# Nonlocal attention and the second MoE's dispatch in one block

## The reference

```python
x = x + nonlocal(_ln_c(x))      # theta, phi, g: 1x1 convolutions 256 -> 128; phi and g on the 2x2 max-pooled image
    m1 = softmax(theta1 @ phi1)                # 4096 queries x 1024 keys
    m2 = m1 @ gi1                              # 4096 x 128
    m4 = conv1x1(m2.reshape(128, 64, 64), wz_w, wz_b)
t = t + moe(_ln_t(t))           # logits = t @ Wg + bg, the two largest, softmax over the two
    out += w_e * (gelu(t @ W1[e] + b1[e]) @ W2[e] + b2[e])     # W1: 256 x 1024, W2: 1024 x 256
```

## Time and profile before

| | us |
|---|---|
| median of 3 runs | 2480.7 (2469.35 to 2482.45) |
| the profiled execution | 2486.87, its span 2485.1 |
| layer1_start | about 1670 to 1758 |
| nonlocal_attention | about 1759 to 1893 |
| dispatch of MoE 1 | about 1894 to 2028 |
| experts of MoE 1 | about 2035 to 2438 |
| combine, output | to 2485 |

### The profile page before, as it was taken

How to read it: one execution, slowest core, us unless ns; L and a number is a source line. 1 busy time by engine, 2 the same in 40 slices (tenths; PEclk the granted TensorE clock), 3 DMA queues, 4 the chain that set the end, 5 groups by cost and what they waited for, 6 DMA issues and landing times. The chain is left out here.

```text
span 2485.1 us, 83832 instructions
## 1 busy us (share of the span) xinstructions
PE 2015.4 (81%) x28694; PEld 1524.5 (61%) x28695; DVE 2062.4 (83%) x3713; ACT 1732.2 (70%) x2708; POOL 790.9 (32%) x604
## 2 busy tenths in 40 slices
PE   6749999999999999999996208856896229999994
PEld 3327666666666766666664206643684129999992
DVE  5779999999999999999997646759797457777775
ACT  5569999999999999999984415537686335555551
POOL 3432124241431331231440553430364532222220
PEclk9869999999999999999997559985997559999996
DMA  2013323232323232323232233442112341111116
GB/s 81 1 34 89 84 77 89 72 92 70 92 71 91 71 90 71 90 72 89 73 85 84 87 131 104 116 126 95 45 68 84 112 135 51 48 47 47 51 44 209
DMA packets 285209, 202.98 MB, mean 82 GB/s; under 512 B 153395, under 2 KB 259846, under 8 KB 284870
## 3 DMA queue, kind: packets, MB, share of 16 engines
q1 hardware_dynamic: 271168, 163.57, 22.8%
q0 software_dynamic: 12960, 35.73, 3.9%
q10 hardware_dynamic: 998, 2.62, 0.3%
HBM read 68.98 MB, written 108.60 MB: 71 GB/s over the span
## 5 line engine op out<-in xcount | busy, mean ns | idle before, releaser
L595 DVE TENSOR_TENSOR plow<-prob 128x1024 f16<-128x1024 f32 (+1 forms) x1024 | 1127.1, 1171 | 3.7 <-ACT prob L506 3.7
L506 ACT ACTIVATE prob<-scores 128x1024 f32<-128x1024 f32 x1024 | 999.5, 1025 | 88.9 <-PE scores L638 58.5
L658 PEld LDWEIGHTS outp<-vs,prob 128*128 128x128 bf16 x7680 | 515.3, 98 | 279.8 <-issue 219.9
L658 PE MATMUL outp<-vs,prob 128*128 (+1 forms) x7680 | 603.6, 193 | 25.0 <-DVE plow L595 12.4
L638 PE MATMUL scores<-qT,kT 128*128 (+1 forms) x2048 | 610.6, 380 | 7.5 <-DMA kT<-shift_rows 2.7
L660 PE MATMUL outp<-vs,plow 128*128 (+1 forms) x7680 | 601.2, 193 | 0.0
L660 PEld LDWEIGHTS outp<-vs,plow 128*128 128x128 f16 x7680 | 502.8, 97 | 57.9
L448 POOL TENSOR_TENSOR osum<-osb 128x128 f32<-128x128 f32 x64 | 269.9, 4217 | 783.4 <-DVE rec L600 783.4
L1476 POOL DMA_INDIRECT expert_rows<-m1eyo,m1edest x71 | 108.0, 1521 | 304.5 <-DVE m1eyo L1448 275.5
L1347 PE MATMUL m1eph<-m1exT,m1ew1c 128*128 128x128 f16 x3408 | 203.4, 220 | 0.3 <-ACT m1exT L1384 0.3
L1347 PEld LDWEIGHTS m1eph<-m1exT,m1ew1c 128*128 128x128 f16 x3408 | 194.5, 98 | 1.0 <-ACT m1exT L1384 0.5
(11 more groups left out here) (393 smaller groups left out, 3335.4 us busy)
## 6 DMA issues: line engine op xcount, KB each, us to landing
sorted_rows<-zero SPq DMA_DIRECT2D x128, 522.0 KB, 4.7
staged<-qk SPq DMA_DIRECT2D x73, 128.0 KB, 2.3
m0exr<-sorted_rows SPq DMA_DIRECT2D x71, 130.5 KB
...
```

Source lines behind the costliest of these rows:

```text
L506: act.activation(prob[g % PBUF][:, :], scores[g % 2][:, :], ACT.Exp, scale=1.0 / (QK_SCALE * QK_SCALE)).then_inc(prob_ready, 1)
L595: dve.tensor_tensor(l[:, 0:n], p[:, 0:n], high(p)[:, 0:n], ALU.subtract).then_inc(low_ready, 1)
L658: pe.matmul(to, high(prob[g % PBUF])[:, cols], v, start=(g == 0 and i == 0 and j == 0), stop=False, skip_group_check=True)
```

## The change

Attention and dispatch become one block, `nonlocal_and_dispatch`. No loop: all 39 ticks (32 and 7 behind them) are written out. A row tile's result is now multiplied by the reciprocal in ACT (`image`, out of PSUM), and the reciprocal is taken by DVE straight behind the exponential (`invert`); `project(r-1)` stands where `project(r)` would, behind `scores`; the bias of the projection is two more one-row matmuls instead of POOL's addition. As soon as four token tiles are final they pass through the dispatch steps: `scales` (the root now by DVE in 13 linked operations instead of ACT), `normed`, `prepare`, `turn_row`, `take`, `mult` (8 matmuls instead of 4), `first_choice`, `second_choice`, `rank`, `places` and POOL's two sends for each tile, 4 to 11 ticks behind the attention. W2 now lies in the room that the attention's operands use, so its 16 parts are loaded and halved only after the last projection, three in each of the ticks 33 to 37 and one in tick 38. The MoE's `b1`, gate and bias loads go to the block's start; `experts` and `combine_experts` stay.

```diff
-def nonlocal_attention(nc, qh, ql, kh, kl, gh, gl, zw, zb_dram, ident32, tok, stats, w1_dram, w1):
+def nonlocal_and_dispatch(nc, qh, ql, kh, kl, gh, gl, zw, zb, prob, pth, ptl, tok, stats, consts, ...):
...
+        TICKS = range(NT + 7)
+        due = lambda r, i: (r - i) // TG if (r - i) % TG == 0 and 0 <= (r - i) // TG < NGR else None
+        w2_before = lambda r: min(NW2, max(0, 3 * (r - NT))) if r < NT + 6 else NW2
...
+            for i in range(NW2):                      # sync
+                if i < KB:
+                    sp.wait_ge(w1_high, 4 * (E_N - 1) + 2 * i + 2)
+                elif i == KB:
+                    sp.wait_ge(w1_split, NT)
+                else:
+                    sp.wait_ge(w2_split, i - 2)
...
+            for r in TICKS:                           # vector
+                if r + LOOKED < NT:
+                    maxima(r + LOOKED)
+                if 1 <= r <= NT:
+                    add(r - 1)
+                if r + 1 < NT:
+                    invert(r + 1)
+                g = due(r, 10)
+                if g is not None:
+                    places(g)
+                g = due(r, 6)
+                if g is not None:
+                    prepare(TG * g)
+                g = due(r, 7)
+                if g is not None:
+                    prepare(TG * g + 2)
+                    prepare(TG * g + 3)
+                g = due(r, 8)
+                if g is not None:
+                    first_choice(g)
+                if 1 <= r <= NT:
+                    gather(r - 1)
+                if r + 2 < NT:
+                    low(r + 2)
+                g = due(r, 4)
+                if g is not None:
+                    scales(g)
+                g = due(r, 6)
+                if g is not None:
+                    prepare(TG * g + 1)
+                g = due(r, 9)
+                if g is not None:
+                    second_choice(g)
+                for i in range(w2_before(r - 1), w2_before(r)):
+                    w2_low(i)
...
+            for r in TICKS:                           # scalar
+                g = due(r, 7)
+                if g is not None:
+                    take(TG * g)
+                    take(TG * g + 1)
+                g = due(r, 8)
+                if g is not None:
+                    take(TG * g + 3)
+                if r + 2 < NT:
+                    high(r + 2)
+                g = due(r, 7)
+                if g is not None:
+                    take(TG * g + 2)
+                if r + LOOKED < NT:
+                    exps(r + LOOKED)
+                if r + 1 < NT:
+                    image(r + 1)
...
+                if r < NT:
+                    w1_to_high(r)
...
+            def times_g(r):                           # tensor
+                pe.wait_ge(lo_ready, r + 1)
+                if r:
+                    pe.wait_ge(m3_ready, r)
+                if r >= 2:
+                    pe.wait_ge(added, r - 1)
...
+            for r in TICKS:
+                if r + LOOKED < NT:
+                    scores(r + LOOKED)
+                g = due(r, 10)
+                if g is not None:
+                    rank(g)
+                g = due(r, 7)
+                if g is not None:
+                    mult(TG * g)
+                    turn_row(TG * g + 1)
+                g = due(r, 8)
+                if g is not None:
+                    mult(TG * g + 3)
+                if 1 <= r <= NT:
+                    project(r - 1)
+                if r + 2 < NT:
+                    turn(r + 2)
+                g = due(r, 7)
+                if g is not None:
+                    mult(TG * g + 1)
+                    turn_row(TG * g + 2)
+                if r + 1 < NT:
+                    times_g(r + 1)
+                g = due(r, 7)
+                if g is not None:
+                    mult(TG * g + 2)
+                    turn_row(TG * g + 3)
+                g = due(r, 6)
+                if g is not None:
+                    turn_row(TG * g)
...
+            for r in range(NT + 11):                  # gpsimd
+                if r < NT:
+                    split(r)
+                if 1 <= r <= NT:
+                    w1_low(r - 1)
+                t = r - 11
+                if t >= 0:
+                    send(t)
```

666 lines of the change are left out of this document (453 added, 213 removed).

## The result

The changed kernel takes 2510.6 us (median of 4 runs, 2506.6 to 2514.9) against 2479.7 for the kernel before: a ratio of 1.0133, 95% interval [1.0114, 1.0151]. Forecast were 2475 us and a small gain. The time lies just inside the range given, but on the other side of the kernel before. Two further comparisons of the same two kernels gave 1.0089 [1.0055, 1.0123] and 1.0104 [1.0082, 1.0127].

The account below looks back on a forecast made before the run. Attention was held bound by TensorE, dispatch by chains of waits. Start-up, joint ticks (21 full ones at 6.7 us) and W2 tail end at 2022 against 2027.2; 2481.6 profiled, less 6.2 to the median, gives 2475 us, range 2446 to 2512.

Parts of the forecast that it names:

- the allowance of 1.1 us a round: Joint ticks, per four: added to 25.7 us for semaphores and GpSimd-VectorE meetings, giving 26.8, or 6.7 a tick.
- the 11.5 us for ticks 29 to 31: End of the attention: three ticks without maxima were to take 11.5 us together.
- the end of the tail: Behind W2's low half 14 at 2009: eight last sends, 10.2 us, and 2 for landing, ending at 2022.
- The bound: Joint block: VectorE bounds by load, 5.65 us a tick, but the engines' program order costs more, 6.7.
- Rival 1: Joint ticks: engines slide over the order, so a tick costs VectorE's load, 5.65 us; 2453 us, chance 0.25.
- The chain of 25.7 us: One group followed through four joint ticks across VectorE, TensorE and ScalarE: 25.7 us, against 22.6 by load.
- rival 2: Joint ticks: GpSimd's W1 low and split stretch threefold beside VectorE, 8.2 us a tick; 2506 us, chance 0.15.
- The clock: Joint ticks, a rival: TensorE falls to 1.2 GHz and needs 9.4 us a tick; 2543 us, chance 0.10.
- 1.00 in the joint loop: Sign named for the forecast: TensorE's granted clock at 1.00 through the joint ticks, against 0.6 for the clock's fall.
- Ticks 4 to 7: 22: First ticks with part of the routing: 22 us, the four-tick chain less first and second choice and rank.
- the tail is what pays: Behind the last projection: all 16 W2 parts, then last sends, end at 2022 against 2027.2, 5 us earlier.
- Rival 4: Joint block: unexplained ScalarE stalls at `take`, 31.7 us in the old dispatch, return; 2505 us, chance 0.05.

Follow-up runs that it names:

- the best order tried: Changed kernel with split scales, addition first, 5 fillers, earlier take and projections, W2 one part a tick with tables between: ratio 1.0038, in another session 0.9998.
- with the dip and the meeting removed: Changed kernel without W1's low halves, with 11 filler matmuls in the gap before `times_g`: ratio 1.0120, median 2486.5 us, five rounds 133.1 us.
- The early projections: Changed kernel with 15 filler matmuls, plus project(30) and project(31) ahead of gate work in tick 31: ratio 1.0119, run-down 23.2 us instead of 29.5.
- the tables between the parts: Changed kernel with filler matmuls, plus one W2 part per tick and the tables' instructions behind single W2 parts: ratio 1.0117, stretch 368.7 us.

## Why the prediction was wrong, point by point

The steps that failed are three terms of the sum: the allowance of 1.1 us a round, the 11.5 us for ticks 29 to 31, and the end of the tail, which lacks GpSimd's `DRAIN`.

- **The bound.** Right in kind: no engine but the order of four ticks sets the time. The tick spacings of the second full round were 8.8, 5.9, 5.3 and 7.8 us, forecast 7.4, 5.2, 6 and 7. Rival 1 (5.65 us a tick) is excluded by every run; the best order tried gave 25.5 us for four ticks.
- **The chain of 25.7 us, plus 1.1.** The chain was right: with the dip and the meeting removed, the rounds at full clock took 26.1 to 26.3 us. It holds link by link in the round from 1887.62 of that run: the mask for `rank` is ready 12.4 us behind the maxima (12.35 in the prediction), the first `take` ends at 19.4 (19.2), the addition behind the projection starts at 20.7 (20.5). The allowance of 1.1 for semaphores and meetings is the mis-sized term. It came to 3.0 us in two executions (28.7 a round) and 3.8 in the first (29.5).
- **POOL and VectorE shut each other out.** I priced it on GpSimd's side only, from the earlier trace rows, and gave VectorE's loss no place in the sum. It was the other way round. GpSimd's subtraction keeps its length: 1155 ns in the changed kernel, 1159 in the earlier trace rows, so rival 2 is false. VectorE loses 1.0 us once a round, in a chain of links that the next tick waits for. The groups on GpSimd:

```profile
L2439 POOL TENSOR_TENSOR m1w<-nd_staged,m1w 128x512 f16<-128x512 f32 x30 | 34.6, 1155 | 21.7 <-ACT m1w L2241 21.7
```

  The rule of the Trainium skill ("SBUF — State Buffer", section "Who interferes with whom") that the engine that comes first holds the ports for its whole instruction is borne out on this side too: the VectorE instruction started 0.01 us after GpSimd's and ended 0.02 us after it. The prediction had bounded this at up to 20 us and left it in the spread; it cost 8 to 11 of the stretch, with the dips that came of it.
- **The clock.** The rival was all or nothing: 1.2 GHz throughout or full speed throughout. What came is between. The clock falls behind the one long gap and is back within a few us; it cost 1.0 to 1.1 us a dip inside the rounds, and 7 to 10 us of the stretch by kernels of different sessions. I had seen that gap and sized it at 2.5 to 2.9 us. The meeting made it 3.56, and where 1.00 in the joint loop was named as the sign of being right, 0.94 to 0.79 was seen.
- **Ticks 4 to 7: 22.** 26.9 us. I took the choices and the rank out of the chain, but `scales` with its meeting and the gap behind it are there already; without W1's low halves these ticks take 24.2.
- **Ticks 29 to 31: 11.5.** The step that failed outright, at 17.5 us. I reckoned that ticks without maxima, scores and exponentials are short, and gave no chain for them. The chain of such a tick holds none of those: it is image, split, project, addition, times_g, and in tick 31 the gate's steps ahead of the projection. The early projections gave back 6.4 us of it.
- **The tail.** Its shape was right: the loads pace the parts (2.39 us a high half instead of 2.3), `places` stands behind low half 14, eight sends of 1.28 follow. The landing took 1.7 us, of the 2 allowed. What the sum lacked is GpSimd's `DRAIN` of 5.28 us behind it. It had only the 2.8 us that the kernel before took from its last W2 part to the next block, and those were the rest of its own `DRAIN`. And the claim that "the tail is what pays" was the wrong way round: last places behind W2's parts, with the sends and the `DRAIN` alone behind them, cost 10 us, as the tables between the parts show.
- **Rival 4.** No such waits came along; ScalarE's waits for `px` are ended by TensorE's transposes, with small sums.
- **The profile against the median.** I took 6.2 us off, since the profiled execution of the kernel before stood so much above its median. It also reached the stretch 6.6 us later than that of the changed kernel did, which is why the profiled executions are 19.7 us apart and the medians 31.

In sum: 25 us too low in rounds and run-down by the profile, 5 in the tail, and the sign follows from the first of these.
